# Attention scores as three rounded products on the four row parts, the causal mask by 32x32 tiles, and one stage order per engine

## The reference, cut to what matters

```python
qkv = layernorm(x) @ W_attn.T + b_attn          # (32, 128, 384)
q, k, v = 16 heads of 8 channels;  q = q * f;  k = k * f      # f depends on position
att = einsum('bhqd,bhkd->bhqk', q, k) / sqrt(8)
att = where(causal, att, -huge);  att = softmax(att)
x = x + (einsum('bhqk,bhkd->bhqd', att, v) merged) @ W_proj.T + b_proj
```

## Time and profile before

| | us |
|---|---|
| median of three runs | 524.39 |
| profiled execution | 523.54 |
| its span, first to last instruction | 521.5 |
| first scores start | 30.0 |
| last scores start | 298.4 |
| first expert tile loaded from | 366.6 |

### The profile page before, as it was taken

The page is one execution under the profiler, slowest core; times in us unless marked ns, Lnnn a source line. Parts: engine busy times, 40 slices in busy tenths (PEclk is TensorE's granted clock), DMA queues, the critical chain, the costliest instruction groups (busy, mean ns, idle before and its releaser), DMA issues. The chain is left out here.

```text
span 521.5 us, 11896 instructions
## 1 busy us (share of the span) xinstructions
PE 443.0 (85%) x3612; PEld 304.7 (58%) x3612; DVE 381.4 (73%) x1236; ACT 271.6 (52%) x887; POOL 273.2 (52%) x368
## 2 busy tenths in 40 slices
PE   2658889998998898998998978659898989989993
PEld 2323455555555555554655555437687878878783
DVE  5653667879979789789789676967576666666685
ACT  1014476775676766666666656552254545545520
POOL 6214262453564855846755655566165555556571
PEclk9978999999999999999999988567899999999998
DMA  7510101001002011010111002512122322323294
GB/s 199 134 42 2 48 8 47 16 10 48 18 23 69 18 46 47 23 63 23 34 58 34 18 29 88 158 42 84 47 79 78 88 80 79 86 77 88 66 335 123
DMA packets 41596, 34.57 MB, mean 66 GB/s; under 512 B 6464, under 2 KB 36432, under 8 KB 41536
## 3 DMA queue, kind: packets, MB, share of 16 engines
q1 hardware_dynamic: 36478, 24.51, 16.5%
q0 software_dynamic: 4320, 8.99, 5.2%
q10 hardware_dynamic: 738, 0.33, 0.2%
HBM read 17.26 MB, written 12.09 MB: 56 GB/s over the span
## 5 line engine op out<-in xcount | busy, mean ns | idle before, releaser
L560 POOL DMA_INDIRECT ys<-ctx_t,xload x71 | 68.6, 966 | 60.5 <-ACT ctx_t L974 58.1
L541 POOL TENSOR_SCALAR_AFFINE_SELECT probs<-probs 128x512 f32<-128x512 f32 x128 | 78.6, 651 | 35.6 <-ACT probs L880 35.6
L1082 DVE TENSOR_REDUCE negmax<-ps_scores 128x4 f32<-128x512 f32 x128 | 81.3, 680 | 16.8 <-PE ps_scores L632 16.1
L880 ACT ACTIVATE probs<-ps_scores 128x512 f32<-128x512 f32 x128 | 69.6, 607 | 33.1 <-PE ps_scores L651 33.1
L534 POOL DMA_INDIRECT xs<-xrow,posu x64 | 63.5, 993 | 22.7 <-issue 14.6
L791 PE MATMUL ps_scores<-wide,xe 128*128 x213 | 68.8, 432 | 0.0
L547 POOL TENSOR_TENSOR x1b<-x,bias 128x128 f32<-128x128 f32 x32 | 14.6, 456 | 77.4 <-DVE x L1103 77.4
L1287 DVE COPY probs<-ps_shared 128x256 f32<-128x256 f32 x71 | 30.1, 425 | 24.9 <-PE ps_shared L799 24.5
L808 PE MATMUL ps_shared<-wd,probs 128*128 x284 | 43.8, 277 | 0.1
L964 ACT ACTIVATE xe<-ps_scores 128x128 fp32r<-128x128 f32 x71 | 19.7, 278 | 44.7 <-PE ps_scores L783 44.7
L632 PE MATMUL ps_scores<-causal,ident 128*128 128x512 bf16 x128 | 42.8, 386 | 0.0
(11 more groups left out here) (215 smaller groups left out, 1040.3 us busy)
## 6 DMA issues: line engine op xcount, KB each, us to landing
xload<-xs SPq DMA_DIRECT2D x71, 66.0 KB, 1.9
wide<-qk SPq DMA_DIRECT2D x64, 64.0 KB, 1.9
wide<-ys SPq DMA_DIRECT2D x8, 512.0 KB, 7.3
ctx_t<-in_ctx SPq DMA_DIRECT2D x32, 64.0 KB, 2.0
out_x<-res SPq DMA_DIRECT2D x8, 256.0 KB, 3.1
ys<-ctx_t,xload POOLq DMA_INDIRECT x71, 2.2
wd<-in_L_ffn_w_down SPq DMA_DIRECT2D x8, 128.0 KB, 3.3
xs<-xrow,posu POOLq DMA_INDIRECT x64, 2.3
```

The lines of the kernel that those rows point to most:

```text
L541: pool.affine_select(out=part, in_=part, compare_op=ALU.is_ge, fill=0.0, base=0, pattern=[[0, HJ], [1, T]], channel_multiplier=-1).then_in ...
L560: pool.indirect_dma_start(out=ys, out_offset=bass.IndirectOffsetOnAxis(ap=xload_i[:, i % XL, C + 1:C + 2], axis=0), in_=ybuf[:, i % 4, :], ...
L880: act.activation(probs[:, b % 2, j * HJ:(j + 1) * HJ, :].rearrange("p a t -> p (a t)"), SC[j][:], ACT.Exp)\
L1082: dve.reduce_max(negmax[:, b % 2, j * HJ:(j + 1) * HJ], SC[j][:].rearrange("p (i t) -> p i t", i=HJ), axis=AX.X, negate=True).then_inc(max ...
```

## The change

Four things.

1. **Products.** DVE writes q and k of a group to `qk32` in fp32. ACT rounds them to fp32r (`round`), POOL subtracts to get the rest (`rest`); both are kept in `qk` and both are placed by DMA. scores and scores_t then take, instead of one fp32 product for each part, three fp32r products: rounded by rounded, rest by rounded, rounded by rest.
2. **Mask.** Instead of one 128x128 by 512 identity matmul per bank, four 32x32 identity tiles per bank, which cover only the columns where the mask can act (4 heads by 128, 96, 64 and 32 keys).
3. **Placing.** `project` on SP becomes `place`, in four parts for a group: k of the first two rows, k of the last two, q of the first two, q of the last two. Each part is 8 DMAs of 32 KB, 32 for a group instead of 8 of 64 KB. `k_heads` and `q_heads` become rings of six rows, cleared in six pieces of 2048 columns instead of four.
4. **Order.** Each engine has its own list. On DVE the clears of `turn_x(0)` now follow `project(0)`. On SP, `turn_max(b)` of a slot stands behind the first two parts of `place` and before the last two. `gate_up(0)` moves from slot 37 to slot 39. The lists are written in short in the diff below: stage, offset, part behind the slash.

```diff
+    "SP": [
+        ("place", 2, 0, 0), ("place", 2, 1, 0), ("turn_max", 1, None, None),
+        ("turn_x2", -5, None, None), ("place", 2, 2, 0), ("place", 2, 3, 0),
+    ],
+    "POOL": [ scatter 0 and norm_x, weights, scatter 1,
+        ("exps", -1, 0, None), ("exps", -1, 1, None), ("exps", -1, 2, None),
+        ("rest", 2, 0, 0), ("attn_out", -4, None, None), ("exps", -1, 3, None), ("rest", 2, 1, 0),
+    ],
+    "PE": [ xproject -5, gate_up -39, turn_max -1, xout -6, turn_x 2 (group), scores 0,
+        turn_x2 -4, turn_y -3, xscores -5, turn_ffn -7, values -2, attn_out -3, project_v 0, router -7,
+        scores_t -1, project 2/0 (group), ranks -12 (group), turn_xprobs -5, project 2/1 (group), tall_sums -2 ],
+    "ACT": [ ..., exps 0, exps 1, turn_xprobs, exps 2, round 2/0, exps 3, turn_max 0, round 2/1, xproject, split ],
+    "DVE": [ xscores -5, row_max 0/2, row_max 0/3, attn_out -3, weights, router -7, project 2/0, route -11,
+        turn_xprobs -5, norm_ffn -6, ranks -12, project 2/1, norm_x_stats 4, norm_xattn -3, split,
+        tall_sums -2, xout -5, turn_x 2 (group), row_max 1/0, row_max 1/1 ],
...
+            def place(g, part):
+                n, half = part // 2, part % 2
+                pair = 2 * g + half
+                slot = pair % (RING // 2)
+                w.ge(qk_split, 2 * g + n + 1)
+                if pair < RING // 2:
+                    w.ge(heads_cleared, 2 * pair + n + 1)
+                w.ge(scored_t, NJ * (2 * pair + 2 - RING))
+                for i in range(HJ):
+                    for a in range(2):
+                        sp.dma_start(heads[i:128:HJ, 2 * slot:2 * slot + 2, a, i, :].bitcast(fp32),
+                                     qk[i:128:HJ, g % 2, 1 - n, a, 2 * half * T:2 * (half + 1) * T]...)
...
+            def rest(g, n):                       # POOL
+                w.ge(qk_rounded, 2 * g + n + 1)
+                pool.tensor_tensor(qk[:, g % 2, 1 - n, 1, :], qk32[:, 1 - n, :], qk[:, g % 2, 1 - n, 0, :].bitcast(fp32), ALU.subtract)
+            def round_qk(g, n):                   # ACT
+                act.activation(qk[:, g % 2, 1 - n, 0, :], qk32[:, 1 - n, :], ACT.Copy).then_inc(qk_rounded, 1)
...
             def scores(b):
-                for j in range(NJ):
-                    pe.matmul(SC[j][:], qk[r, g % 2, 0, ts], k_heads[r, g % 2, :, ts], start=True, stop=False)
-            def causal_mask(b, j):
-                pe.matmul(SC[j][:], ident16[:], causal[:].rearrange("p a t -> p (a t)"), start=False, stop=True).then_inc(scored, 1)
+                for m, h in ((0, 0), (1, 0), (0, 1)):
+                    for j in range(NJ):
+                        pe.matmul(SC[j][:], qk[r, g % 2, 0, m, ts], k_heads[r, slot, h, :, :]..., start=(m + h == 0), stop=True)
+                for j in range(NJ):
+                    for a in range(4):
+                        keys = T - 32 * a
+                        mm = pe.matmul(SC[j][32 * a:32 * (a + 1), :]...[:, :, 32 * a:], ident16[r, r],
+                                       causal[r, a, 32 * a:]...broadcast_to([32, HJ, keys]), start=False, stop=True)
+                    mm.then_inc(scored, 1)
             def scores_t(b):
-                    pe.matmul(SC[j][:], qk[r, g % 2, 1, ts], q_heads[r, g % 2, :, ts], start=False, stop=True).then_inc(scored_t, 1)
+                for m, h in ((0, 0), (1, 0), (0, 1)):
+                    for j in range(NJ):
+                        mm = pe.matmul(SC[j][:], qk[r, g % 2, 1, m, ts], q_heads[r, slot, h, :, :]..., start=False, stop=(h == 1))
...
             def turn_x(g):                        # DVE
                 if g == 0:
-                    clear(q_heads[:, 0])
-                    clear(k_heads[:, 1])
-                    clear(q_heads[:, 1])
+                    clear(q_heads[:, 0:2].bitcast(fp32))
+                    for i in range(2, RING, 2):
+                        clear(k_heads[:, i:i + 2].bitcast(fp32))
+                        clear(q_heads[:, i:i + 2].bitcast(fp32))
                     late_setup()
```

More of the change, by code:

```diff
@@ L51 @@
 AHEAD = 3
+RING = 6
 XL = 8
[L57 to L98, removed]
@@ new lines, with timeline @@
+LATE = {"weights": NJ, "split": 2, "gate_up": 1}
+GROUP_STAGES = ("norm_x_stats", "rstd_x", "norm_x", "turn_x", "project", "round", "rest", "place", "route", "ranks")
+ENTRIES = [entry for entries in ORDER.values() for entry in entries]
+FIRST_SLOT = -max(ahead for _, ahead, _, _ in ENTRIES)
+END_SLOT = B - min(ahead for name, ahead, _, _ in ENTRIES if name not in LATE)
+def timeline(engine):
+    for s in range(FIRST_SLOT, END_SLOT):
+        for name, ahead, part, which in ORDER[engine]:
+            b = s + ahead
+            if 0 <= b < LATE.get(name, B) and (which is None or b % GB == which):
+                yield (name, b // GB if name in GROUP_STAGES else b) + (() if part is None else (part,))
@@ L121 @@
 W_LOADS = 15
-BANK = {"turn_xprobs": 3, "turn_x": 1, "turn_y": 2, "xproject": 0, "attn_out": 2, "values": 0, "xscores": 1, "turn_ffn": 3, "xout": 3, "turn_max": 2, "project_v": 1, "tall_sums": 1, "router": 3, "turn_x2": 0, "ranks": 0, "project": (0, 1)}
+BANK = {"turn_xprobs": 2, "turn_x": 1, "turn_y": 2, "xproject": 0, "attn_out": 2, "values": 0, "xscores": 1, "turn_ffn": 3, "xout": 3, "turn_max": 2, "project_v": 1, "tall_sums": 1, "router": 3, "turn_x2": 0, "ranks": 0, "project": (0, 3)}
 SETUP_FILLS = (1, 1, 1, 1)
@@ L128, in bank_fills @@
     count, fill = list(SETUP_FILLS), {}
-    for item in [x for s in range(FIRST_SLOT, END_SLOT) for x in timeline(s)]:
+    for item in timeline("PE"):
         name = item[0]
@@ L364, in scores_free, with run @@
                     self.ge(maxed if name == "scores" else exped, NJ * (b + 1))
-            def run(self, stages):
-                for s in range(FIRST_SLOT, END_SLOT):
-                    for name, *args in timeline(s):
-                        if name in stages:
-                            stages[name](*args)
+            def run(self, engine, stages):
+                for name, *args in timeline(engine):
+                    stages[name](*args)
         def put_bank(item):
@@ L421, in turn_max @@
                              max_rows[:].bitcast(fp32)).then_inc(max_placed, 16)
-            w.run(dict(turn_x2=turn_x2, project=project, turn_max=turn_max))
+            w.run("SP", dict(turn_x2=turn_x2, place=place, turn_max=turn_max))
             w.bank_read(("values", B - 1))
@@ L762, in down @@
                 mm.then_inc(down_done, 1)
-            w.run(dict(turn_x=turn_x, project=project, project_v=project_v, scores=scores, causal=causal_mask, turn_max=turn_max, scores_t=scores_t,
+            w.run("PE", dict(turn_x=turn_x, project=project, project_v=project_v, scores=scores, turn_max=turn_max, scores_t=scores_t,
                        values=values, tall_sums=tall_sums, turn_y=turn_y, attn_out=attn_out, turn_x2=turn_x2,
```

177 lines of the change are left out of this document (135 added, 42 removed).

## The result

The kernel after takes 561.11 us, median of four runs (556.91 to 565.32), beside 524.14 (522.32 to 524.8) for the kernel before: a ratio of 1.0685, 95% interval 1.0615 to 1.0754. The medians are of all timed executions, while this ratio and those further down are formed without the executions that fell into the chip's slower state, here one of the four. The forecast was 522.7, and its range ended at 534. The profiled execution has a span of 558.5 us, 37.0 more than before.

The account below looks back on a forecast made before the run. TensorE and VectorE were both near full, so order within a slot decided, with SP's queue as a new cost. Gains of 15.7 us and costs of 14 summed to -1.7: median 524.39 becomes 522.7, range 507 to 534.

Parts of the forecast that it names:

- TensorE's part: Scores, mask and transposed scores of each row: 2.91 us becomes 2.06, 0.85 less.
- D: Slot piece from subtraction through transposed scores until the first exp: 1.39 us now, 1.33 forecast.
- rival of small matmuls: In scores, masks and transposed scores, small matmuls cost what they save: +8 us, 531; chance 0.10.
- the loop without copies: Steady attention group of four rows, SP's waits apart: 34.4 us from slots of 7.74, 8.5, 9.29 and 8.89, saving 1.6.
- B: Slot piece of VectorE's four maxima with a small reduction between, 2.69 us; part of the route and ranks slots' bound.
- the start's mechanisms: Before the first subtraction: 32 copies precede the first max row, landing at 44.6; clears alone give 42.0; cost 5.0 us.
- SP's queue: SP's issuing: 32 copies a group at 0.60 us; 22.1 needed against 22.0 available, 0.3 a group, longer waits in groups 1, 2.
- rival 2: SP's queue: above 0.61 us a copy, scores_t of rows 4g waits for max_row; 535 at 0.65; chance 0.18.
- Rival 4: Attention slots: TensorE idles about 1 us twice a slot and the clock falls, +16 us, 539; chance 0.04.
- 3.2 per tenth: SP's queue: each tenth of a microsecond a copy above 0.60 adds 3.2 us for each of 8 groups.
- the end: Drain of the last rows: -2 us, from -5 to +2; moving gate_up(0) gains nearly nothing.
- Rival 1: SP's queue stays hidden if a half-size copy costs 0.47 us or less: 511; chance 0.30.

Follow-up runs that it names:

- e7: Kernel before, with only the mask changed to sixteen 32x32 tiles, one bank's four at a time between other stages: 542.21 us, 1.0231 of the kernel before.
- e12: Kernel after, with merged copies (16 of 64 KB a group), route behind the second exp, two of five start clears behind row 1's maxima: 505.64 us, 0.9643 of before.
- e1: Kernel after, with the max_row copy issued by ScalarE right behind its copy of the maxima instead of by SP: 552.64 us, 1.0344 of the kernel before.
- e3: Kernel after, without the copies of the rests (16 a group); the third product repeats the second: 543.21 us, 1.0133 of the kernel before.
- e5: Kernel after, with rounded and rest of two rows laid together, 16 copies of 64 KB a group instead of 32 of 32 KB: 534.83 us, 1.006 of before.
- e4: Kernel before, with each 64 KB copy of q or k cut into four of 16 KB, same bytes: 615.71 us, 1.1495 of the kernel before.
- e15: Repeat of e12's kernel (merged copies, route behind second exp, two clears behind row 1's maxima) on a chip where before takes 531.67: 529.84 us, 0.9975 of before.
- e16: Kernel before, unchanged, run again for its trace on the chip where it takes 531.67 us: 530.87 us, 1.0003.
- e11: Kernel after with merged copies and route behind the second exp, with gate_up(0) back in slot 37 instead of 39: 540.18 us, 1.0109 of the kernel before.
- e14: Repeat of e8's kernel (merged copies, route behind the second exp) on a chip where the kernel before takes 531.67: 536.01 us, 1.0073 of before.
- e17: e15's kernel with four full 128x128 identity mask matmuls behind the scores instead of the sixteen tiles: 531.57 us, 0.9997 of the kernel before.
- e8: Kernel after with merged copies, plus ScalarE's route moved behind the second exp instead of ahead of the first: 535.14 us, 1.0035 of the kernel before.
- e9: Kernel after with merged copies and route behind the second exp, with four full 128x128 masks instead of sixteen tiles: 541.76 us, 1.0139 of the kernel before.

## Why the prediction was wrong

**Right: TensorE's part.** 2.07 for 2.06 a row; mask tiles 0.36 where 0.5 was taken, products 0.90 and 0.81 where 0.78 was. D was put at 1.33, though its own rows give 1.22 (0.34, 0.78 and 0.10); it measured 1.36 (223.56 to 224.92). The rival of small matmuls that eat their own gain falls, for tiles that stand together; e7 shows what it looks like where they don't.

**Right in the sum: the loop without copies.** 34.4 was forecast for a group and e12 shows 34.46. In the slots the errors cancel: free 7.74 forecast, 8.08 measured (7.60 to 7.61 before the late stages set in); project 8.5 and 8.59; route 9.29 and 8.26; ranks 8.89 and 9.63. The step "with B these slots last 9.29 and 8.89 whatever TensorE does" was wrong slot by slot: VectorE's full stretch begins in the route slot and ends in the ranks slot, and with DVE's list reordered only their sum is bound, 18.18 forecast, 17.89 measured. The kernel before shows the same, 8.68 and 9.38 from scores to scores (191.84, 200.52, 209.90). From the first subtraction to the last scores e12 takes 248.11 for 258.86: 10.8 gained, where the terms of the forecast without copies come to 13.7.

**Right: the start's mechanisms, and gate_up.** 32 copies from 23.55, all ahead of the first max row; first subtraction at 46.06 for 44.6, since a copy took 0.643 and not 0.60. Clears alone were to give 42.0; with the max row or half the copies out of the way e1, e3 and e5 show 43.05, 42.68 and 43.04.

**Wrong: "SP's queue".** The step that failed is "I take 0.60 for the new copies of half the size", and what follows, "22.1 ... against 22.0 ... 0.3 a group". This sum balanced two numbers of 22 us to within 0.1, on a price known to no better than 0.1 by 32. A copy took 0.68 in the steady phase, inside the bounds of 0.30 to 0.70 that the text itself set. It wasn't dearer for its 64 pieces: a single one takes 0.60, just as before. But 0.60 as the length of a burst divided by four is short, since the first of those four takes only 0.47 to 0.52; from start to start it is 0.64, 1.3 more for 32, and the two long copies add 1.4. The kernel before has long ones too: two of its bursts of four last 3.10 and 3.62 (at 83.74 and 191.17). From the first copy to the landing there were 25.3 us, not 22.1 (2.7 for the copies, the rest landing and gaps), and there was room for 21.3 (25.3 less the wait of 4.0), not 22.0. Thus the wait is 3.3 to 4.1 in each of the seven groups, and not 4.5 and 3.0 in two of them and 0.3 in the others: rival 2's mechanism, at its place. By e12 the split copies cost 46.3 us between the first subtraction and the last scores (294.42 against 248.11), where the sum put 9.0. The decisive point, 0.61, stood in the text, and 0.70 was worked out nowhere: by its own 3.2 us for each tenth, 0.70 gives 26 us more, 548, far outside of a range that ended at 534. The chance of 0.18 was as far off: the longest row, eight copies in 5.00, said 0.625, already beyond the 0.61 that decides.

**Missed: the wait brings the clock down.** Rival 4 set the price of idle time apart, at 0.04, and for idling of 1 us. Behind each of the seven long waits the subtraction takes 0.80, and 0.50 behind the four short ones of 0.2 to 1.1. The wait of 4.00 is followed by 5.66 us at 0.50, in which what takes 3.53 in e12 (207.19 to 210.72, L716 to the next scores) takes 5.61 (245.34 to 250.95): 2.1 more for each group. 4.0 and 2.1 are the 6.1 between 40.59 and 34.46. So the term "3.2 per tenth" lacked about 2 us for each group once TensorE waits for 4 us at a stretch. It is a sum and not a factor: in e4 a wait of 7.40 is followed by 5.39 us at 0.50 (255.61 to 261.00), no more than here.

**Undersized: the end.** -2.0 forecast, -5.1 measured (-8.2 in e12, -2.3 in e15 against e16). gate_up isn't the cause (e11); which of the reordered stages is was not tried. In this stretch the granted clock is 0.91 before, 0.93 after and 0.94 in e12, and TensorE is busy for 187.4, 181.7 and 180.2 us, so the gain goes along with the clock; what raised that is open.

Rival 1 (SP hidden, 511, 0.974 of the median) did not come about by its mechanism, a cheaper copy. The merged layout reaches its outcome by halving the number: 0.9643, of which 1.0% are the moved clears, where the kernel before takes 525 us, and 0.9975 where it takes 532. Two slips in the text, 17.7 for 17.6 and 534 for 535, change nothing.

## What to carry to other kernels

Count DMAs for each queue, not bytes: multiply the queue's time per DMA by the number in a period, and compare that with the room before the next small transfer that an engine waits for. Read the time per DMA from start to start in a long burst (0.64 here), with the long ones in it (0.68), and not from a short one (0.60); where the two are within a tenth, take the dearer price and forecast both outcomes. If data must be split for arithmetic, lay the parts side by side in memory, so that one DMA carries them. And where TensorE waits out of full clock as long as it does here, price the half clock behind the wait too: 4.0 us of waiting cost 6.1.

## What the runs showed of the hardware

- SP's price for issuing an on-chip copy hardly depends on its size: a median of 0.594 us for 64 KB in 32 pieces (the kernel before, e12), 0.594 for 16 KB in 32 pieces (e4), 0.600 for 32 KB in 64 pieces (after), 0.58 for the 8 KB max row, with 0.04 to the next. In each kernel some copies take longer (1.1 to 1.7 in 13 of 256 in the kernel after, 1.3 and 1.8 in 2 of 64 in the kernel before); why was not looked into.
- Chips differ, and not by a factor. On three of them (e1 to e4 with e14 to e17, e5 to e8, e9 to e11) the kernel before took 531 to 536 us instead of 524 to 525, in e16 all of it behind the attention phase (233.5 against 223.1). The new version lost 3.4% more there (0.9975 against 0.9643 for the same code). In its attention phase, TensorE's handoff to ScalarE took 1.2 us instead of 0.31 in one or two slots of four, at full clock. These late handoffs begin with the first scatter, and GpSimd's indirect DMA stands beside the one shown (207.72 above). What ties the two is open: no run took the scatter away, and with full masks (e17) this handoff is on time and the groups are no shorter.
- Masks of four, eight and sixteen 32x32 tiles take 0.31, 0.32 and 0.36 us, one over the full array 0.22, each with the step to the next full-array matmul (e7, after, before).
